# Differential attention in a four-layer network: ScalarE's order inside a unit, second exponentials ahead of the copy of turned probabilities

## The chip, the core and the metric

The kernel is one program on one core of a Trainium2 chip. The time is that of one execution on the device, in microseconds (us). The engines named here are TensorE (PE in the profile, PEld for its weight loads), VectorE (DVE), ScalarE (ACT), GpSimd (POOL) and SyncE (SP), which starts the DMA transfers. Each engine works through its own list of instructions in order; they meet only at semaphores.

## The reference, cut to what matters

The network is four layers of attention and feed-forward on x of 8 x 256 x 256 (float32), each followed by a layer norm. The change lies in the fourth attention, which is differential: two softmaxes per head, their difference weighted by lambda, and a softmax of that difference again.

```python
energy = jnp.einsum('bqhad,bkhad->bahqk', qd, kd)          # a = 0, 1; 16 heads, d = 16
energy = jnp.where(causal, NEG, energy)
scores = jax.nn.softmax(energy / np.sqrt(D), axis=-1)       # the first exponentials
...
diff = scores[:, 0] - lam * scores[:, 1]
diff = jnp.where(causal, NEG, diff)
diff = jax.nn.softmax(diff, axis=-1)                        # the second exponentials
att = jnp.einsum('bhqv,bvhd->bqhd', diff, v)
att = att * jax.lax.rsqrt(jnp.mean(att * att, axis=-1, keepdims=True) + EPS) * rms_w
```

## The kernel before, in words

The eight stages of the network run one after the other; `l3_attention` is the seventh. It goes over the 8 batch elements ("batches"). A batch is 8 units, i = 0 to 7: unit i takes the score half a = i % 2 of the four heads r = i // 2 (one head r of each of four groups g). Work is staged over units, so that each engine's list for unit i holds pieces of several units:

- TensorE, `scores(b, i)` (L1911, matmuls at L1922 and L1925): scores of unit i into the four PSUM banks S. There is one set S, so it waits on `p_exp`, which counts the first exponentials of the unit before. Then, at even i, `values` (L1939, matmuls L1946 and L1949) of a head finished earlier; then a `piece` of the next batch's projections (L1861 keys, L1868 queries, L1876 values) or, at i = 0, the output projection of two batches before (L1970); then `turn(b, i, 0)` and `turn(b, i, 1)` (L1936), which transpose the second probabilities of unit i - 4, two heads' worth, into PSUM banks PT[0] and PT[1]; then at even i `turn_back` (L1956).
- VectorE: `maxima` (L2221) of the scores, `second_maxima` (L2237), the ratios, at even i `values_out` (L2253), the rotated projections (L2182, L2185), its share of the copies, `out_of_psum` (L2248, PT[1]), at i = 6 ahead of it the norm of the batch before (`norm_2`, from L2269), and at i = 0 the addition of the projected output to x (L113).
- GpSimd: mask (L2046), `difference` (L2056, L2059) and `second_bias` (L2068), the bias nb2 of the second exponentials.
- ScalarE, per unit: `exponentials` of unit i, twice (L2113; the last one signals `p_exp`), at i = 7 `output` (L2139), then `out_of_psum` for unit i - 4 (L2124: the copy of PT[0] into `pt`, signals `pt_even`) and `second` for unit i - 3 (L2133: four second exponentials, signals `p_ready`).

Who waits for ScalarE's two signals: `turn(b, i, 0)` waits on `p_ready` of the second exponentials that ScalarE makes in unit i - 1, and also on `pt_even` of the copy that it makes in unit i - 1, since PT[0] must be free. `values(b, i)` waits on `pt_even` of the copy in unit i - 1, and not on `p_ready`. ScalarE's copy itself waits on `pt_ps` (the turn of the same unit), its second exponentials on `nb_ready` from GpSimd's L2068.

The batches are an opening (batch 0, where the copy begins at unit 4 and the second exponentials at unit 3), a second pass (batch 1), five turns of a loop (batches 2 to 6), the last batch 7, and a closing pass that has no new scores: on ScalarE copies at units 0 to 3 and second exponentials at units 0 to 2.

Of the kernel before, what the change touches and what calls it, by code (L numbers as in the profile page):

```python
# [1754 lines left out]
def l3_attention(nc, c, x_sb, mv, xT, w, psum):  # L1755
# [10 lines left out]
    with ExitStack() as ctx:  # L1766
# [71 lines left out]
        def live(i, lag, opening, closing):  # L1838

            return i >= lag if opening else i < lag if closing else True  # L1840

        def part(i):

            return slice(2 * (i % 2), 2 * (i % 2) + 2)

        with nc.Block() as block:
            @block.sync
            def _(sp):
                sp.dma_start(xc[:, :, :], xT[:, :, 0:T]).then_inc(x_staged, 16)
                with sp.Fori(0, B - 1) as b:  # L1850
                    sp.wait_ge(piece_ps, b * NQ + 10)
                    sp.dma_start(xc[:, :, :], xT[:, :, bass.ds(b * T + T, T)]).then_inc(x_staged, 16)
# [245 lines left out]
            @block.scalar  # L2098
            def _(act):
                nc.scalar.preload_act_table(ACT.Exp)  # L2100
                act.wait_ge(set_up, 2)
                nc.scalar.activation(lam[:, :, :], lam[:, :, :], ACT.Exp).then_inc(lam_ready, 1)
                act.sem_inc(pt_even, 1)

                def exponentials(b, i, pair, opening):
                    r, a = i // A, i % A
                    if pair == 0 and not opening:
                        act.wait_ge(pt_ps, b * NU * 2 + 4 * r - 12)
                    act.wait_ge(nm_ready, 2 * (b * NU + i) + pair + 1)
                    for g in range(2 * pair, 2 * pair + 2):  # L2110
                        for t in range(TT):
                            k = slice(t * P, t * P + (t + 1) * P)
                            last = nc.scalar.activation(pr[:, r, a, g, k], S[:, g, k], ACT.Exp, bias=nm[:, i % 2, g, t:t + 1],  # L2113
                                                        accum_out=sums[:, r, a, g, t:t + 1])
                    if pair == 1:
                        last.then_inc(p_exp, 1)

                def out_of_psum(b, i, opening):
                    s = b * NU + i - 4
                    r, g = (i - 4) // 2 % R, part(i - 4).start  # L2120
                    if not (opening and i - 4 < 4):
                        act.wait_ge(av_ps, b * R + (i - 4) // 2 - 1)
                    act.wait_ge(pt_ps, 2 * s + 1)
                    nc.scalar.activation(pt[:, r % 2, g, :], PT[0][:, 0:3 * P], ACT.Copy).then_inc(pt_even, 1)  # L2124

                def second(b, i):
                    s = b * NU + i - 3
                    r, heads = (i - 3) // 2 % R, part(i - 3)
                    act.wait_ge(nb_ready, s + 1)
                    for g in range(heads.start, heads.stop):  # L2130
                        for t in range(TT):
                            k = slice(t * P, t * P + (t + 1) * P)
                            last = nc.scalar.activation(pr[:, r, 1, g, k], pr[:, r, 0, g, k], ACT.Exp, bias=nb2[:, r, g, t:t + 1],  # L2133
                                                        scale=rec[:, r, 0, g, t:t + 1])
                    last.then_inc(p_ready, 1)

                def output(b):
                    act.wait_ge(oT_ps, b + 1)
                    nc.scalar.activation(oT[:, :, :], OT.rearrange("p (k t) -> p k t", k=KD), ACT.Copy).then_inc(oT_ready, 1)  # L2139

                def sequence(b, opening=False, closing=False):
                    for i in range(NU):
                        if not closing:
                            exponentials(b, i, 0, opening)
                            exponentials(b, i, 1, opening)
                        if i == 7 and not opening:
                            output(b - 1)
                        if live(i, 4, opening, closing):
                            out_of_psum(b, i, opening)
                        if live(i, 3, opening, closing):  # L2150
                            second(b, i)

                sequence(0, opening=True)
                with act.Fori(0, B - 1) as b:
                    sequence(b + 1)
                sequence(B, closing=True)

            @block.vector
# [743 lines left out]
```

## Time and profile before

| what | value |
|---|---|
| median of 3 runs | 2773.51 us (2773.32 to 2775.98) |
| the profiled execution, its own time | 2775.95 us |
| its span, first to last instruction | 2774.1 us |
| the fourth attention, first to last exponentials L2113 | 1863.3 to 2290.0 us of the span |
| the five loop batches, unit 0 to unit 0 | 54.7 us each |
| ACT, DVE, POOL busy in batch 3 (54.67 us) | 44.3, 41.1, 40.2 us |

The profiled execution's own time stands 2.4 us above the median of the runs. Times inside the trace are microseconds from the start of its span. "Idle before" names the engine whose signal ended the wait of an instruction. In a timeline a row is one or several instructions of one line in a row: start, duration, engine, line, output<-input, count, and in brackets the wait ahead of it.

### The profile page before, as it was taken

How to read it: one execution, taken by the hardware profiler on the slowest of the kernel's cores; microseconds unless marked ns; L12 is line 12 of the kernel's file. 1: busy time of each engine (PE TensorE's matmuls, PEld its weight loads, DVE VectorE, ACT ScalarE, POOL GpSimd, SP SyncE). 2: the span in 40 equal slices, each digit the busy share in tenths (PEclk: the TensorE clock that was granted, in tenths of full speed). 3: DMA queues.
4: the chain of work that ended last, by engine and by line, in shares of the span. 5: the costliest groups of instructions: out<-in, count | busy, mean ns of one | idle time of the engine just before them, and what ended most of it. 6: DMA issues, size and time to landing. Idle time of an engine off the chain costs nothing. (4 is left out here: it accounts for less than half of the span.)

```text
span 2774.1 us, 42332 instructions
## 1 busy us (share of the span) xinstructions
PE 2418.6 (87%) x13892; PEld 1890.7 (68%) x13892; DVE 1898.9 (68%) x4354; ACT 1389.3 (50%) x3744; POOL 500.6 (18%) x477
## 2 busy tenths in 40 slices
PE   6997999979999999999699788977777775999998
PEld 5665566657777777777577666855555554888887
DVE  3664588867655665566554577866777775788887
ACT  4664477765445444545322214327878783333332
POOL 2442200020000000000022100007777771000000
PEclk9998999989999999999899999989898876999999
DMA  4001000001001100110200000010000003222222
GB/s 162 11 11 62 1 1 0 0 34 35 22 12 34 34 23 11 34 34 26 110 0 0 0 0 0 1 52 5 9 4 4 4 4 140 72 64 72 70 64 59
DMA packets 43902, 88.79 MB, mean 32 GB/s; under 512 B 7328, under 2 KB 20128, under 8 KB 42272
## 3 DMA queue, kind: packets, MB, share of 16 engines
q1 hardware_dynamic: 43808, 87.58, 9.6%
q8 instruction: 54, 0.88, 0.1%
q14 instruction: 40, 0.33, 0.0%
HBM read 78.65 MB, written 2.36 MB: 29 GB/s over the span
## 5 line engine op out<-in xcount | busy, mean ns | idle before, releaser
L2113 ACT ACTIVATE l3a_pr<-psum,l3a_nm 128x128 f32<-128x128 f32 (+1 forms) x512 | 207.3, 430 | 73.3 <-DVE l3a_nm L2221 73.3
L1099 ACT ACTIVATE l1a_pr<-psum,l1a_nb,l1a_rq 128x128 f32<-128x128 f32 (+1 forms) x256 | 127.4, 510 | 80.3 <-DVE l1a_nb L1185 74.5
L2221 DVE TENSOR_REDUCE l3a_nm<-psum 128x2 f32<-128x256 f32 (+1 forms) x256 | 124.7, 549 | 54.8 <-PE psum L1925 54.5
L1361 POOL TENSOR_TENSOR l1f_acc<-l1f_t 128x512 f32<-128x512 f32 x4 | 6.3, 1571 | 838.6 <-DVE l1f_t L1427 838.6
L2513 ACT ACTIVATE l3f_sg<-psum 128x512 f32<-128x512 f32 x96 | 57.4, 598 | 193.4 <-PE psum L2465 193.4
L2463 PE MATMUL psum<-l3f_x_hi,l3f_w_hi 128*128 128x512 f32 x384 | 151.8, 395 | 1.7 <-DVE l3f_w_lo L2549 1.7
L2464 PE MATMUL psum<-l3f_x_lo,l3f_w_hi 128*128 128x512 f32 x384 | 151.5, 395 | 0.0
L2465 PE MATMUL psum<-l3f_x_hi,l3f_w_lo 128*128 128x512 f32 x384 | 150.3, 392 | 0.0
L113 DVE TENSOR_TENSOR x_sb<-psum,x_sb 128x512 f32 (+3 forms) x44 | 36.7, 833 | 162.3 <-PE psum L1038 104.9
L2046 POOL TENSOR_TENSOR l3a_pr<-l3a_pr,w_l3a_mask 128x1024 f32<-128x1024 f32 x32 | 75.5, 2360 | 316.4 <-ACT l3a_pr L2113 316.4
L372 POOL TENSOR_TENSOR l0a_pr<-l0a_pr,l0a_rec 128x256 f32<-128x256 f32 (+1 forms) x128 | 101.7, 826 | 142.6 <-DVE l0a_rec L462 142.6
L2133 ACT ACTIVATE l3a_pr<-l3a_pr,l3a_nb,l3a_rec 128x128 f32<-128x128 f32 (+1 forms) x256 | 120.2, 568 | 3.3 <-POOL l3a_nb L2068 3.3
L2497 ACT ACTIVATE l3f_w_hi<-w_l3f_all 128x768 fp32r<-128x768 f32 x96 | 81.3, 848 | 80.6 <-PE psum L2482 80.3
L1001 PE MATMUL psum<-l1a_kT,l1a_qT 128*128 128x128 f32 (+1 forms) x512 | 100.8, 342 | 22.7 <-ACT l1a_pr L1099 15.8
L1038 PE MATMUL psum<-l1a_kT,l1a_ko 128*128 128x256 f32 x512 | 112.6, 381 | 6.1 <-ACT l1a_ko L1088 6.1
L2059 POOL TENSOR_TENSOR l3a_pr<-l3a_pr 128x768 f32<-128x768 f32 x64 | 115.8, 1810 | 5.0
L2480 PE MATMUL psum<-l3f_w_hi,l3f_h_hi 128*128 128x256 f32 x384 | 109.1, 284 | 2.4 <-DVE l3f_h_lo L2599 2.4
L1038 PEld LDWEIGHTS psum<-l1a_kT,l1a_ko 128*128 128x128 f32 x512 | 96.6, 190 | 20.4 <-issue 7.6
L2113 ACT ACTIVATION_READ_ACCUMULATOR l3a_pr<-psum,l3a_nm 128x1 f32 x512 | 110.3, 215 | 0.0
L392 ACT ACTIVATE l0a_pr<-psum,l0a_nm 128x128 f32<-128x128 f32 (+1 forms) x256 | 103.6, 437 | 10.6 <-DVE l0a_nm L449 10.2
L2482 PE MATMUL psum<-l3f_w_hi,l3f_h_lo 128*128 128x256 f32 x384 | 108.9, 284 | 0.0
L2481 PE MATMUL psum<-l3f_w_lo,l3f_h_hi 128*128 128x256 f32 x384 | 108.8, 283 | 0.0
(447 smaller groups left out, 7275.2 us busy)
## 6 DMA issues: line engine op xcount, KB each, us to landing
l1a_kT<-l1a_o_dram SPq DMA_DIRECT2D x64, 256.0 KB, 2.7
l3f_cbuf<-l3f_c_rows SPq DMA_DIRECT2D x64, 192.0 KB, 2.9
w_l3f_all<-l3f_all_dram SPq DMA_DIRECT2D x1, 9216.0 KB, 24.8
l3f_cbuf<-l3f_c_rows SPq DMA_DIRECT2D x64, 128.0 KB, 3.0
w_l0f_w<-l0f_w_dram SPq DMA_DIRECT2D x2, 2048.0 KB, 10.2
l3f_cbuf<-l3f_c_rows SPq DMA_DIRECT2D x64, 64.0 KB, 2.6
w_l1f_all<-l1f_all_dram SPq DMA_DIRECT2D x1, 2560.0 KB, 8.7
cf_sb<-xT SPq DMA_DIRECT2D x9, 256.0 KB, 2.5
```

Source lines behind the costliest of these rows:

```text
L1038: last = mm(PT[0][:, t * D:(t + 1) * D], oT[:, h, t * P:(t + 1) * P], wo[:, h, :], start=(h == 0), stop=(h == H - 1))
L1099: last = nc.scalar.activation(pr[:, n % 2, i, s], S[n % 2][:, i, s], ACT.Exp, bias=nb[:, n % 2, t, i:i + 1], scale=rq[:, t, 2 * n + i:2 * ...
L2059: nc.gpsimd.tensor_tensor(pr[:, r, 0, heads, :], pr[:, r, 0, heads, :], pr[:, r, 1, heads, :], ALU.add).then_inc(dif_ready, 1)
L2113: last = nc.scalar.activation(pr[:, r, a, g, k], S[:, g, k], ACT.Exp, bias=nm[:, i % 2, g, t:t + 1], accum_out=sums[:, r, a, g, t:t + 1])
L2133: last = nc.scalar.activation(pr[:, r, 1, g, k], pr[:, r, 0, g, k], ACT.Exp, bias=nb2[:, r, g, t:t + 1], scale=rec[:, r, 0, g, t:t + 1])
L2221: last = nc.vector.tensor_reduce(nm[:, i % 2, 2 * pair:2 * pair + 2, t], S[:, 2 * pair:2 * pair + 2, t * P:t * P + (t + 1) * P], AX.X, ALU ...
L2463: mm(bk[n % 2], hi, x_hi[:, k, chunk], start=(k == 0), stop=False)
L2464: mm(bk[n % 2], hi, x_lo[:, k, chunk], start=False, stop=False)
L2465: last = mm(bk[n % 2], lo, x_hi[:, k, chunk], start=False, stop=(k == KD - 1))
L2480: mm(Y[b % 2][:, t, :], h_hi[:, n % 2, tokens], hi, start=False, stop=False)
L2481: mm(Y[b % 2][:, t, :], h_hi[:, n % 2, tokens], lo, start=False, stop=False)
L2482: last = mm(Y[b % 2][:, t, :], h_lo[:, n % 2, tokens], hi, start=False, stop=(e == NH - 1 and t % 2 == 1))
```

## The change

In each unit ScalarE's program now calls `second` ahead of `out_of_psum`. Nothing else is edited; the other engines' lists are the same as before.

```diff
                         if i == 7 and not opening:
                             output(b - 1)
+                        if live(i, 3, opening, closing):
+                            second(b, i)
                         if live(i, 4, opening, closing):
                             out_of_psum(b, i, opening)
-                        if live(i, 3, opening, closing):
-                            second(b, i)
```

ScalarE's list in a unit of the loop, the difference from before to after (l3a_pt<-psum is the copy of turned probabilities; l3a_pr<-l3a_pr,l3a_nb,l3a_rec are the second exponentials; L2122 and L2123 are the copy's waits):

```order
+L2133 ACTIVATE l3a_pr<-l3a_pr,l3a_nb,l3a_rec 128x128
+L2133 ACTIVATE l3a_pr<-l3a_pr,l3a_nb,l3a_rec 128x256
+L2133 ACTIVATE l3a_pr<-l3a_pr,l3a_nb,l3a_rec 128x128
+L2133 ACTIVATE l3a_pr<-l3a_pr,l3a_nb,l3a_rec 128x256
 L2122 REGISTER_ALU
 L2123 ISA
 L2124 ACTIVATE l3a_pt<-psum 128x384
-L2133 ACTIVATE l3a_pr<-l3a_pr,l3a_nb,l3a_rec 128x128
-L2133 ACTIVATE l3a_pr<-l3a_pr,l3a_nb,l3a_rec 128x256
-L2133 ACTIVATE l3a_pr<-l3a_pr,l3a_nb,l3a_rec 128x128
-L2133 ACTIVATE l3a_pr<-l3a_pr,l3a_nb,l3a_rec 128x256
```

The four second exponentials have moved from behind the copy to ahead of it; the copy, with its waits, now stands last in the unit.

ScalarE's list from unit 7 of the last batch into the closing pass, before (L2139 is the copy of the turned output, L2154 the end of the loop's code):

```order
L2139 ACTIVATE l3a_oT<-psum 128x512
L2124 ACTIVATE l3a_pt<-psum 128x384
L2133 ACTIVATE l3a_pr<-l3a_pr,l3a_nb,l3a_rec 128x128
L2133 ACTIVATE l3a_pr<-l3a_pr,l3a_nb,l3a_rec 128x256
L2133 ACTIVATE l3a_pr<-l3a_pr,l3a_nb,l3a_rec 128x128
L2133 ACTIVATE l3a_pr<-l3a_pr,l3a_nb,l3a_rec 128x256
L2154 REGISTER_ALU
L2154 COMPARE_AND_BRANCH
L2124 ACTIVATE l3a_pt<-psum 128x384
```

The same place in the changed kernel:

```order
L2139 ACTIVATE l3a_oT<-psum 128x512
L2133 ACTIVATE l3a_pr<-l3a_pr,l3a_nb,l3a_rec 128x128
L2133 ACTIVATE l3a_pr<-l3a_pr,l3a_nb,l3a_rec 128x256
L2133 ACTIVATE l3a_pr<-l3a_pr,l3a_nb,l3a_rec 128x128
L2133 ACTIVATE l3a_pr<-l3a_pr,l3a_nb,l3a_rec 128x256
L2124 ACTIVATE l3a_pt<-psum 128x384
L2154 REGISTER_ALU
L2154 COMPARE_AND_BRANCH
L2133 ACTIVATE l3a_pr<-l3a_pr,l3a_nb,l3a_rec 128x128
```

At the seam the copy of unit 7 now stands behind four second exponentials, and the closing pass begins with second exponentials and not with a copy.

## Rows read from the trace of the kernel before

**Rows 1.** The page: the span.

```profile
span 2774.1 us, 42332 instructions
```

**Rows 2.** Waits between 1880 and 2310 us: waiter, releaser: total us, times, longest.

```profile
ACT l3a_pr L2113 <- DVE l3a_nm L2221: 57.3, 59, 3.1
...
ACT l3a_pt L2124 <- PE psum L1936: 22.0, 17, 3.9
PE psum L1922 <- ACT l3a_pr L2113: 22.0, 18, 3.2
```

**Rows 3.** Stretches batch by batch (3 and 5): length, busy times, clock, DMA.

```profile
2021.75:2076.42 54.67, 41.29 (x349) 29.34 (x350) 41.12 (x104) 44.30 (x170) 40.15 (x38) 0.91 0.01 5
...
2131.12:2185.77 54.65, 44.07 (x349) 31.46 (x350) 41.19 (x104) 44.30 (x169) 40.19 (x38) 0.84 0.01 5
```

**Rows 4.** Timeline, batch 4, end of unit 1 to unit 2, full clock.

```profile
2085.79 0.20 POOL L2068 TENSOR_TENSOR l3a_nb<-l3a_nm,l3a_rec 128x4 f32<-128x4 f32 x1
2085.80 0.53 ACT L2124 ACTIVATE l3a_pt<-psum 128x384 f32<-128x384 f32 x1
2086.17 1.89 ACT L2133 ACTIVATE l3a_pr<-l3a_pr,l3a_nb,l3a_rec 128x128 f32<-128x128 f32 x4
...
2087.41 0.64 PE L1946 MATMUL psum<-l3a_pt,l3a_va 128*32 128x256 f32 x8
...
2090.03 0.82 PE L1936 MATMUL psum<-cf_sb,l3a_pr 128*128 128x128 f32 x6
...
2092.54 0.55 DVE L2248 COPY l3a_pt<-psum 128x384 f32<-128x384 f32 x1
...
2092.75 0.43 PE L1956 MATMUL psum<-cf_sb,l3a_ots 128*128 128x128 f32 x2 [1.90 <-DVE l3a_k L2182]
```

**Rows 5.** Timeline, batch 5, the same place, half clock.

```profile
2143.32 3.21 PE L1861 MATMUL psum<-xT,w_l3a_k 128*128 x8
...
2146.37 0.82 PE L1936 MATMUL psum<-cf_sb,l3a_pr 128*128 128x128 f32 x6
...
2147.45 0.43 PE L1956 MATMUL psum<-cf_sb,l3a_ots 128*128 128x128 f32 x2 [0.26 <-DVE l3a_k L2182]
```

**Rows 6.** Timeline, end of unit 5: batch 1, last row batch 7.

```profile
1950.27 1.86 ACT L2133 ACTIVATE l3a_pr<-l3a_pr,l3a_nb,l3a_rec 128x128 f32<-128x128 f32 x4 [1.06 <-POOL l3a_nb L2068]
...
1950.39 0.64 PE L1946 MATMUL psum<-l3a_pt,l3a_va 128*32 128x256 f32 x8
...
1952.04 0.35 ACT L2113 ACTIVATE l3a_pr<-psum,l3a_nm 128x128 f32<-128x128 f32 x1
...
2278.34 1.87 ACT L2133 ACTIVATE l3a_pr<-l3a_pr,l3a_nb,l3a_rec 128x128 f32<-128x128 f32 x4 [0.84 <-POOL l3a_nb L2068]
```

**Rows 7.** Timeline, unit 7 of the last batch and the closing pass.

```profile
2290.41 0.54 ACT L2124 ACTIVATE l3a_pt<-psum 128x384 f32<-128x384 f32 x1
...
2291.05 1.08 PE L1946 MATMUL psum<-l3a_pt,l3a_va 128*32 128x256 f32 x8 [2.84 <-ACT l3a_pt L2124]
...
2296.24 0.69 DVE L113 TENSOR_TENSOR x_sb<-psum,x_sb 128x512 f32<-128x512 f32 x1 [3.20 <-PE psum L1970]
...
2297.44 1.00 DVE L2237 TENSOR_REDUCE l3a_nm<-l3a_pr 128x2 f32<-128x256 f32 x2
...
2298.70 0.20 POOL L2068 TENSOR_TENSOR l3a_nb<-l3a_nm,l3a_rec 128x4 f32<-128x4 f32 x1
...
2304.79 0.88 PE L1936 MATMUL psum<-cf_sb,l3a_pr 128*128 128x128 f32 x6 [1.37 <-ACT l3a_pr L2133]
```

**Rows 8.** Stretches unit by unit: units 5 and 7 of batches 3, 5.

```profile
2055.26:2061.41 6.15, 6.12 (x56) 4.64 (x56) 4.88 (x11) 5.57 (x21) 5.47 (x5) 0.85 0.12 43
...
2068.43:2076.42 7.99, 5.99 (x46) 3.79 (x46) 4.24 (x10) 5.93 (x23) 6.00 (x5) 0.79 0.00 0
...
2164.64:2172.40 7.76, 7.76 (x56) 5.83 (x56) 4.94 (x11) 5.57 (x22) 5.46 (x5) 0.67 0.10 34
...
2179.42:2185.77 6.35, 5.05 (x50) 3.33 (x49) 4.23 (x10) 5.93 (x22) 6.02 (x5) 0.96 0.00 0
```

## The prediction

> **What bounds the kernel now.** I read the page first, for the span [rows 1]; the change touches only the fourth attention, about a sixth of it, so I read the rest there. Next the waits of that stretch [rows 2]. They show a ring: nearly every unit's exponentials L2113 wait for VectorE's maxima L2221 (59 waits, 57.3 us), VectorE waits for TensorE's scores, and these wait for ScalarE's exponentials only in 18 cases (22.0 us on the matmuls). In most other units TensorE comes to `scores` late through its own list. Third, the stretches by batch [rows 3]: a loop batch lasts 54.7 us, in which ScalarE is busy 44.3 us and every other engine less, so nobody is full. The time is a ring of signals, and what counts is not how much ScalarE does but when its two signals come. Last I read the timeline unit by unit, which gives the ends of the waits.
>
> One unit of ScalarE's tail, in [rows 4]: the copy starts at 2085.80, the second exponentials at 2086.17, that is 0.37 later (the copy's 0.53 overlaps the next start), and they last 1.89. So the tail is 0.37 + 1.89 = 2.26 us after the exponentials end, in either order. Before, `pt_even` comes at +0.53 and `p_ready` at +2.26. After, `p_ready` comes at +1.89 and `pt_even` at about +2.26: roughly 1.7 us later, and later still where the bias of GpSimd is not there.
>
> **The change part by part.** No instruction is added or removed; five per unit change places, and no DMA is among them.
>
> What could gain. `turn(b, i, 0)` needs both signals of the unit before, so it starts at the end of the tail in either order; 0.37 us of earlier `p_ready` is worth nothing. The other gain is where the copy sat waiting for its turn: 22.0 us in 17 waits [rows 2], mostly in units 3 and 5. Now the second exponentials fill that time. But the next exponentials wait for VectorE's maxima, and those for scores that TensorE issues behind its projections and turns, none of which waits for ScalarE there. So the tail ends sooner and ScalarE waits longer at L2113. I take 0 us; the bound is 22.0, if everything behind moved with it.
>
> What can lose. `values` at even units needs only `pt_even`. In [rows 4] it starts at 2087.41. After: the tail starts at 2085.80, but the bias L2068 ends at 2085.99, so the second exponentials start near 2086.04, and the copy ends 2.26 later, 2088.3. `values` slips by 0.9 us, and so do the keys and turns behind it: the turn that starts at 2090.03 and lasts 0.82 would end near 2091.8. VectorE takes it up only at 2092.54, and `turn_back` at 2092.75 waits for VectorE's L2182. So 0.7 us of slack is left and the slip is swallowed: 0 us in batches 1 to 4. What is late next is only TensorE's own keys.
>
> In batches 5 and 6 the same place runs at the lower clock: eight key matmuls take 3.21 us, turn starts at 2146.37, and `turn_back` follows after a wait of only 0.26 [rows 5]. A slip of 0.9 meets that 0.26 of idle, and about 0.2 comes back because the shifted keys run partly past the slow stretch. About 0.45 us stays, twice: 0.9 us. The bounds are 0, and 0.9 in each of the batches 1 to 6, 5.4 us, if the slack is not there.
>
> In unit 5 of batch 1 ScalarE is late through GpSimd: the copy ran ahead and then the second exponentials waited 1.06 us for the bias, from 1950.27 for 1.86 us, and the next exponentials start at 1952.04 without a wait [rows 6]. Now the copy comes behind them, so it adds its 0.37 to the path: the exponentials of unit 6 start 0.4 us later. `values` slips from 1950.39 to about 1952.6, by 2.2, but VectorE reads its result only later. I take 0.4 us (0 to 2.2). Batch 7 has the same case [rows 6], with the lower clock a little behind it, so the turns of unit 6 may hold up VectorE's norm as well: 0.6 us (0.4 to 2.0).
>
> The closing pass has no exponentials to hide behind. At its head `values` waits 2.84 us for the copy of unit 7, which starts at 2290.41 and lasts 0.54, and goes at 2291.05 [rows 7]. Moved behind the second exponentials, that copy ends at 2290.41 + 2.26 = 2292.7, and `values` starts 1.7 us later, and with it the output projection and VectorE's addition L113 at 2296.24. Some comes back: the second exponentials that `turn` waits for in unit 1 of this pass stood behind a copy that waited for the turn of unit 0; in the new order they are made while TensorE still projects. What then comes last is VectorE's list behind L113. L113 moves to 2297.9, the second maxima L2237 start 1.2 us after it and the bias L2068 starts 1.26 after those [rows 7], so this bias is ready at about 2300.6. Two tails of 2.26 follow, to 2305.1, and up to 0.5 for the last bias, 2305.6. The last turn, which needs the second of these tails, started at 2304.79 [rows 7], so the end comes 0.3 to 0.8 later. I take 0.8 us, the last bias being behind VectorE's whole list (bounds 0 and 1.7, nothing given back).
>
> The sum: 0.9 + 0.4 + 0.6 + 0.8 = 2.7 us. On the profiled execution that is 2775.95 + 2.7 = 2778.65; this execution stood 2.4 above the median, so for the median 2773.51 + 2.7 = 2776.2 us. All lower bounds give 2773.9, all upper ones 5.4 + 2.2 + 2.0 + 1.7 = 11.3, so 2784.8. What a measurement of this kernel tells from no change is about 0.2%, 5.5 us.
>
> **A rule weighed.** The rows show that the lower clock matters by place. Batch 3 had a granted clock of 0.91 and batch 5 one of 0.84, and they last 54.67 and 54.65 us [rows 3]: equal, because in batch 3 unit 7 was slow (7.99 us at 0.79) and unit 5 fast (6.15 at 0.85), and in batch 5 unit 7 fast (6.35 at 0.96) and unit 5 slow (7.76 at 0.67) [rows 8]. One slow stretch on the path costs 1.6 us and each batch has one. The Trainium skill, "TensorE: Matmul & The Clock Gate", section "HAM oscillation — how this bites in real kernels", says that matmuls which keep pausing for something fall back to the half clock, over and over. By that rule the new pause ahead of `values` speaks against the change, and each loop batch could catch a second slow stretch, which would give the result of the second rival below; by the rows a pause moves slow stretches more than it adds them.
>
> **The rivals.**
> 1. *The `values` slip is not swallowed* (slower). The slack of 0.7 us in [rows 4] holds only if VectorE's list there stays late. If it does not, the upper end of that term counts, 5.4 + 0.4 + 0.6 + 0.8 = 7.2: 2780.7 us. For it: 0.26 us in [rows 5]. Against: 1.90 us of wait in [rows 4].
> 2. *Two slow stretches a batch* (slower): 1.6 us in each of five loop batches, 8.0 on top of 1.8: 2783.3 us. For it: longer pauses of TensorE. Against: batches 3 and 5 traded one for the other.
> 3. *No slow stretch on the path* (faster): the slip moves TensorE's bursts so that the lower clock falls on neither unit 5 nor unit 7: 1.6 us less in each of five batches, 2773.5 + 1.8 - 8.0 = 2767.3 us. It decides from 5 of 5 batches on, since with 4 (6.4 less 1.8) the gain is under 5.5 us.
> 4. *The whole is hidden*: the closing pass gets back at its turns what it lost at its head and the rest is under the maxima's waits: 2773.5 us. The change then does nothing.
>
> **How the numbers follow.** The forecast 0.60; rival 1 has 0.11, rival 2 0.12, rival 3 0.09, rival 4 0.08. The forecast's own range is 2774 to 2779. The forecast and rival 4 are within 0.2% (0.68), rivals 1 and 2 slower (0.23), rival 3 faster (0.09). The range for 8 in 10 goes from 2770 (halfway into rival 3, two or three batches) to 2783, up to rival 2.
>
> **What would show it in the profile after.** The waits of L2124 for L1936 nearly gone in the loop (from 22.0 us to a few), and the waits of L2113 for L2221 longer, or less if the units grew; new waits of L1946 for L2124, of 0.9 us at unit 2 in each batch and 2.2 us at unit 6 of batch 1; `turn_back` at unit 2 at the same distance from the exponentials as before; unit 5 of batch 1 longer by 0.4 us; the first `values` of the closing pass waiting 1.7 us more, and its last turn 0.8 us later. Wrong would be: a loop batch that no longer lasts 54.7 us, either way.

## The result, and the profile after

The changed kernel takes 2782.11 us, median of 19 runs (2775.44 to 2786.7), the one before 2774.86 (19 runs, 2763.33 to 2780.23). The ratio is 1.0026 with an interval of 1.0018 to 1.0034: slower by 7.2 us, 5.0 to 9.4. The forecast was 2776.2, a change of 2.7 us and with it most of the chance on "within 0.2%". The range and the sign hold. The size does not, and 0.26% lies outside the "within 0.2%" that had 0.68 of the chance.

The profiled execution of the changed kernel has this span, 4.7 us above [rows 1]:

```profile
span 2778.8 us, 42332 instructions
```

The waits in the fourth attention, the changed kernel, 1880 to 2315 us (waiter, releaser: total us, times, longest):

```profile
ACT l3a_pr L2113 <- DVE l3a_nm L2221: 72.6, 53, 3.0
...
PE psum L1922 <- ACT l3a_pr L2113: 23.3, 18, 3.3
...
PE psum L1946 <- ACT l3a_pt L2124: 21.4, 14, 5.9
...
ACT l3a_pr L2133 <- POOL l3a_nb L2068: 9.2, 10, 1.8
...
ACT l3a_pt L2124 <- PE psum L1936: 6.9, 4, 4.0
```

Against [rows 2]: the copy's wait for its turn went from 22.0 us to 6.9, and ScalarE's wait for the maxima from 57.3 to 72.6. The idle time of ScalarE was mostly moved. New is the third row: `values` L1946 waits 21.4 us for the copy (in the same view of before 2.8 us, once).

Where the time went is seen in the lengths of batches, from the start of the first exponentials L2113 of one batch to those of the next, read from the timelines of both (batch 7 up to the start of its last unit):

| us | batch 0 | 1 | 2 | 3 | 4 | 5 | 6 | 7 | whole, to the end of the last L2113 | from there to the last L113 |
|---|---|---|---|---|---|---|---|---|---|---|
| before | 50.67 | 53.02 | 54.73 | 54.67 | 54.70 | 54.65 | 54.64 | 46.34 | 426.75 | 30.05 |
| changed | 50.68 | 55.95 | 55.48 | 54.99 | 53.71 | 55.28 | 56.33 | 49.36 | 435.11 | 30.12 |

The exponentials' part is 8.4 us longer, 2.9 of them in batch 1, 2.4 in the loop, 3.0 in batch 7. The closing pass, where the forecast put 0.8, is not longer by more than 0.1. No loop batch but batch 3 is still within 0.5 us of 54.7, which is the sign of being wrong that the prediction named. The stages ahead of this one took 3.2 us less in this execution, which the change doesn't touch.

Unit 2, batch 3, of the changed kernel, first the timeline:

```profile
2033.58 0.46 ACT L2124 ACTIVATE l3a_pt<-psum 128x384 f32<-128x384 f32 x1
2034.09 1.08 PE L1946 MATMUL psum<-l3a_pt,l3a_va 128*32 128x256 f32 x8 [0.80 <-ACT l3a_pt L2124]
...
2035.53 3.78 PE L1861 MATMUL psum<-xT,w_l3a_k 128*128 x8
...
2039.11 1.39 PE L1936 MATMUL psum<-cf_sb,l3a_pr 128*128 128x128 f32 x6
...
2040.33 0.38 PE L1956 MATMUL psum<-cf_sb,l3a_ots 128*128 128x128 f32 x2
```

then that unit and the whole batch as stretches (length, busy times, granted clock, DMA):

```profile
2035.06:2043.00 7.94, 7.94 (x53) 6.09 (x46) 4.97 (x13) 5.44 (x22) 5.53 (x7) 0.67 0.00 0
...
2022.21:2077.20 54.99, 43.01 (x365) 30.62 (x358) 41.36 (x104) 44.24 (x169) 40.16 (x38) 0.88 0.01 5
```

`values` waits about the forecast pause (0.80 us). But then `values`, the keys and the turns run at the lower of TensorE's two levels, 1.2 and not 2.4 GHz: the keys take 3.78 us, the turns 1.39 and not 0.82 as in [rows 4], and unit 2 is 7.94 us long at a clock of 0.67. Only `turn_back` (0.38 us) is at the high level again. The same unit in the kernel before:

```profile
2034.61:2040.78 6.17, 4.28 (x38) 3.26 (x37) 4.77 (x13) 5.44 (x22) 3.85 (x5) 1.00 0.00 0
```

The Trainium skill, "TensorE: Matmul & The Clock Gate", section "HAM oscillation — how this bites in real kernels", tells of matmuls that pause for a transfer in every step of a loop and fall back to the half clock each time; its waits are several times as long as this one. The trace agrees in that a low clock goes with the new pause. It does not show the pause as the whole reason. In batch 4 the new pause is the 0.75 us before 2089.09, and the clock had fallen at 2088.0 already, as the row of `values` and two stretches ahead of it show:

```profile
2089.09 1.08 PE L1946 MATMUL psum<-l3a_pt,l3a_va 128*32 128x256 f32 x8 [0.75 <-ACT l3a_pt L2124]
```

```profile
2087.00:2088.00 1.00, 1.00 (x20) 0.62 (x16) 0.81 (x5) 1.00 (x3) 1.00 (x1) 1.00 0.00 0
2088.10:2089.00 0.90, 0.24 (x2) 0.00 (x0) 0.90 (x1) 0.90 (x3) 0.90 (x1) 0.50 0.00 0
```

What differs is how long it stayed low. In batches 3, 4 and 6 it stayed low through the keys (3.78 us) and into the turns. In batches 2 and 5 it was back during the keys (3.13 and 2.88 us), as it was in the kernel before in batches 5 and 6 (3.21 and 3.17), where unit 2 lasted 6.17 and 6.18 us all the same.

A second thing shows in unit 5 of batch 5, the changed kernel:

```profile
2168.20 0.20 POOL L2068 TENSOR_TENSOR l3a_nb<-l3a_nm,l3a_rec 128x4 f32<-128x4 f32 x1
...
2168.44 1.86 ACT L2133 ACTIVATE l3a_pr<-l3a_pr,l3a_nb,l3a_rec 128x128 f32<-128x128 f32 x4 [1.45 <-POOL l3a_nb L2068]
2170.21 0.47 ACT L2124 ACTIVATE l3a_pt<-psum 128x384 f32<-128x384 f32 x1
2170.73 1.08 PE L1946 MATMUL psum<-l3a_pt,l3a_va 128*32 128x256 f32 x8 [2.20 <-ACT l3a_pt L2124]
...
2172.17 1.54 PE L1936 MATMUL psum<-cf_sb,l3a_pr 128*128 128x128 f32 x6
...
2173.82 0.20 DVE L2269 TENSOR_SCALAR psum<-l3a_vv 128x32 int32<-128x32 int32 x1 [1.09 <-PE psum L1936]
```

The bias from GpSimd is late, the second exponentials wait 1.45 us for it, the copy stands behind them, `values` waits 2.20, the turns run at the low clock, and VectorE's norm L2269, which is queued ahead of the next maxima, waits 1.09 for the turn. The forecast had this chain in batches 1 and 7 only. In batch 1 of the changed kernel it did not come: units 4, 5 and 6 last 7.34, 5.83 and 7.21 us there, against 5.88, 6.54 and 6.65 before.

The seam and the closing pass, changed kernel (against [rows 7]):

```profile
2295.54 1.89 ACT L2133 ACTIVATE l3a_pr<-l3a_pr,l3a_nb,l3a_rec 128x128 f32<-128x128 f32 x4
...
2297.29 0.52 ACT L2124 ACTIVATE l3a_pt<-psum 128x384 f32<-128x384 f32 x1
...
2297.91 1.08 PE L1946 MATMUL psum<-l3a_pt,l3a_va 128*32 128x256 f32 x8 [5.95 <-ACT l3a_pt L2124]
...
2310.85 0.84 PE L1936 MATMUL psum<-cf_sb,l3a_pr 128*128 128x128 f32 x6 [0.93 <-ACT l3a_pt L2124]
...
2312.50 0.64 PE L1946 MATMUL psum<-l3a_pt,l3a_va 128*32 128x256 f32 x8 [0.81 <-DVE l3a_pt L2248]
```

### The profile page after: what moved, and what is told of

It is laid out like the page before. It is cut to its first block and busy times, and to the rows that moved or that the text cites. A ratio compares the mean times of both kernels' runs of the same rounds, so it can differ in the third digit from the quotient of the medians.

```text
span 2778.8 us, 42332 instructions
## 1 busy us (share of the span) xinstructions
PE 2417.4 (87%) x13892; PEld 1888.0 (68%) x13892; DVE 1900.3 (68%) x4354; ACT 1387.8 (50%) x3744; POOL 500.6 (18%) x477
## 5 line engine op out<-in xcount | busy, mean ns | idle before, releaser
L2113 ACT ACTIVATE l3a_pr<-psum,l3a_nm 128x128 f32<-128x128 f32 (+1 forms) x512 | 207.0, 429 | 91.7 <-DVE l3a_nm L2221 91.7
L2513 ACT ACTIVATE l3f_sg<-psum 128x512 f32<-128x512 f32 x96 | 57.3, 597 | 192.5 <-PE psum L2465 192.5
L113 DVE TENSOR_TENSOR x_sb<-psum,x_sb 128x512 f32 (+3 forms) x44 | 36.7, 834 | 161.2 <-PE psum L1038 104.9
L2113 ACT ACTIVATION_READ_ACCUMULATOR l3a_pr<-psum,l3a_nm 128x1 f32 x512 | 110.5, 216 | 0.0
```

## The experiments

All times are medians; a ratio is against runs of the kernel before on the same chip. A "part" is the time from the first to the last L2113 in the run's own profile, 426.75 us before and 435.11 changed. It is read from one execution, and in some kernels it does not say the same as the median. Unit lengths are distances between first exponentials.

**Which units.** ScalarE's program asks in each unit which call comes first; the condition is the only difference between the four kernels (`i % 2 == 1`, `i % 2 == 0`, `i == 1`, `i != 1`).

```diff
+                        first = i % 2 == 1
+                        if first and live(i, 3, opening, closing):
+                            second(b, i)
                         if live(i, 4, opening, closing):
                             out_of_psum(b, i, opening)
-                        if live(i, 3, opening, closing):
+                        if not first and live(i, 3, opening, closing):
                             second(b, i)
```

Odd units:

> Second exponentials ahead of the copy in odd units only (1, 3, 5, 7), as before in even ones. The copies whose signal the next unit's values wait for are just those of the odd units. Theory A, the later pt_even delays values at even units and above all at unit 2: the whole loss stays, +6 to +9 us against the kernel before. Theory B, it is the order in general (ScalarE's tail, in every unit): about half, +3 to +4 us.

Even units:

> Second exponentials ahead of the copy in even units only. The copies of even units gate only the turn of the next unit, which needs both signals anyway. Theory A: no change, within 2 us of the kernel before. Theory B, the order in general: about half of the loss, +3 to +4 us.

Unit 1 alone:

> Second exponentials ahead of the copy in unit 1 of each batch alone. Theory A with its place (unit 1 to 2, where TensorE goes on to the keys): +4 to +8 us, the larger part of the loss; the keys of unit 2 run at the lower clock in most batches and unit 2 lasts over 6.9 us in place of 6.2. Theory C, the loss is in units 5 and 7, where GpSimd's bias is late and the copy is put on the path: within 2 us of the kernel before.

All but unit 1:

> Second exponentials ahead of the copy in every unit but unit 1. Theory A with its place: 0 to +3 us, only the terms of unit 5 in batches 1 and 7 (1 us together) and of the closing pass are left. Theory C: the whole loss, +6 to +9 us.

| kernel | median | ratio (interval) | part |
|---|---|---|---|
| odd units | 2783.98 | 1.0038 (1.0024 to 1.0052) | 435.11 |
| even units | 2772.53 | 0.9992 (0.9983 to 1.0001) | 426.77 |
| unit 1 alone | 2770.44 | 0.9987 (0.9978 to 0.9996) | 423.20 |
| all but unit 1 | 2780.63 | 1.0019 (1.0010 to 1.0028) | 428.73 |

The first two rule out theory B: the odd swap repeats the changed kernel batch by batch (55.95, 55.46, 54.99, 53.73, 55.26, 56.32, 49.37 us from batch 1 on), the even swap the kernel before (53.01, 54.74, 54.69, 54.70, 54.65, 54.64, 46.35). Only the copies whose signal `values` waits for count. The last two contradict the place I had given: by the ratios, unit 1 swapped alone makes the kernel 3.6 us faster, and without it 5.3 us of loss remain. The unit lengths say why in part. With unit 1 alone, unit 2 is long as forecast in batches 2 to 5 (6.85, 7.83, 7.94, 7.84 us), but not in batch 6, where the same pause costs nothing:

```profile
2191.77 0.64 PE L1946 MATMUL psum<-l3a_pt,l3a_va 128*32 128x256 f32 x8 [0.83 <-ACT l3a_pt L2124]
...
2192.55 1.99 PE L1861 MATMUL psum<-xT,w_l3a_k 128*128 x8
```

and unit 2 as a stretch:

```profile
2192.73:2198.91 6.18, 5.20 (x41) 4.07 (x42) 4.78 (x13) 5.45 (x21) 3.85 (x5) 1.00 0.00 0
```

A pause of 0.83 us stands ahead of `values`, the clock is 1.00 and unit 2 lasts 6.18 us. So a pause of this length does not always bring the low clock. And in the loop the slow stretches in units 4 and 5 are missing or shorter (in batch 4, 6.59 and 5.85 in place of 7.38 and 7.80). The parts do not add up: -3.55 with unit 1 alone and +1.98 with the rest do not make +8.36. In the kernel without unit 1 the part (+1.98) also says less than the ratio (5.3 us); in its profiled execution the stages behind this attention took 5.8 us more than before, so where the remaining loss lies is not shown.

**The wait alone, on TensorE.** ScalarE as before; `values` waits for the signal that comes last.

```diff
                         if done:
...
+                            if turning:
+                                pe.wait_ge(p_ready, b * NU + i - 3)
                             values(b, i)
```

> ScalarE's order as in the kernel before; TensorE's values alone waits, at even units, also for p_ready of ScalarE's unit before, the signal that now comes last. Theory A, all of the loss comes from the later start of values: as the changed kernel, +6 to +9 us, with the same unit lengths. Rival, the loss is ScalarE's (the copy put behind a late bias, the copy on the path to the next exponentials): under +3 us.

Median 2780.37, ratio 1.0024 (1.0011 to 1.0037): 5.4 us slower (medians), within the interval as much as theory A wanted. But its profiled execution, 2776.9 us, is among the fastest of its 12 runs (2771.57 to 2787.5), its part is 425.26 us, shorter than before, and the unit lengths are not those of the changed kernel; from the end of the part to the last L113 it took 33.51 and not 30.05. Unit 2 is long as in theory A (8.11, 6.93, 7.83, 7.14, 7.91 us in the loop). The run supports that the wait on TensorE is enough to cost something; where it costs in the slower runs, no trace shows.

**Pause or delay.** Two kernels with the same six extra transposes of the unit matrix ahead of `values` at unit 2, in the changed kernel, where they fill the pause, and in the kernel before, where they only delay `values`.

```diff
+                            if i == 2:
+                                for _ in range(6):
+                                    nc.tensor.transpose(OT[:, T:T + P], c["id"], c["id"])
                             values(b, i)
```

Changed kernel, filled:

> The changed kernel with six extra transposes of the unit matrix ahead of values at unit 2 (about 0.8 us of matmul in place of the wait; extra work, the output is not touched by it). Clock theory: with the pause filled the keys run at the full clock, unit 2 is back near 6.2 us in most batches, and the time changes by more than 3 us against the changed kernel, in a direction that the order of slow stretches in the later units decides. Rival, a plain delay: unit 2 stays at 6.9 to 7.9 us and the time is that of the changed kernel, +6 to +9 us on the one before.

Kernel before, delayed:

> The kernel before with the same six transposes ahead of values at unit 2: a delay of values by 0.8 us without a pause. Clock theory: unit 2 stays at about 6.2 us, the slack in front of turn_back takes the delay, within 2 us of the kernel before. Rival, a plain delay of 0.8 us is enough to lengthen unit 2: unit 2 at 6.9 us or more in the loop and +3 us or more.

Filled, the changed kernel takes 2775.89 us, ratio 1.0001 (0.9992 to 1.0010), part 428.16; the delayed one 2774.33, 0.9997 (0.9987 to 1.0007), part 426.75, every batch within 0.03 us of before. Unit 2 of batch 3 in the filled kernel, the timeline (L1990 are the extra transposes):

```profile
2034.24 0.82 PE L1990 MATMUL psum<-cf_sb 128*128 128x128 f32 x6
2035.22 0.64 PE L1946 MATMUL psum<-l3a_pt,l3a_va 128*32 128x256 f32 x8 [0.17 <-ACT l3a_pt L2127]
...
2036.01 2.00 PE L1861 MATMUL psum<-xT,w_l3a_k 128*128 x8
2037.84 0.82 PE L1936 MATMUL psum<-cf_sb,l3a_pr 128*128 128x128 f32 x6
...
2039.66 0.43 PE L1956 MATMUL psum<-cf_sb,l3a_ots 128*128 128x128 f32 x2 [0.99 <-DVE l3a_k L2185]
```

and that unit as a stretch:

```profile
2036.20:2042.38 6.18, 5.18 (x41) 4.06 (x41) 4.78 (x13) 5.44 (x22) 3.85 (x5) 1.00 0.00 0
```

The keys take 2.00 us and not 3.78, the clock is 1.00, and `turn_back` has 0.99 us of the slack that the forecast counted on. The loop batches are 54.59 to 54.64 us long again. So the delay of `values` costs nothing at unit 2 in the loop, as forecast (0.9 us of it here, 0.65 in the delayed kernel); the pause does, through the clock. 7.0 of the 8.4 us of the part go with it. In batch 1 unit 2 still takes 7.31 us in place of 6.09. What stays is 1.4 us, in batch 7 (47.74 us against 46.34), where units 5 and 6 last 6.69 and 7.68 us against 6.32 and 6.64. There the late bias sits ahead of the copy, and the norm behind the turn, as in batch 5 above:

```profile
2279.70 1.86 ACT L2136 ACTIVATE l3a_pr<-l3a_pr,l3a_nb,l3a_rec 128x128 f32<-128x128 f32 x4 [1.23 <-POOL l3a_nb L2071]
2281.47 0.47 ACT L2127 ACTIVATE l3a_pt<-psum 128x384 f32<-128x384 f32 x1
2282.04 1.08 PE L1946 MATMUL psum<-l3a_pt,l3a_va 128*32 128x256 f32 x8 [1.94 <-issue]
...
2285.13 0.19 DVE L2272 TENSOR_SCALAR psum<-l3a_vv 128x32 int32<-128x32 int32 x1 [1.10 <-PE psum L1936]
```

(L2136, L2127 and L2272 are the second exponentials, the copy and the norm there.)

**Keys ahead of `values`.** In the changed kernel the `piece` of unit 2 is called before `values`.

```diff
+                        if i == 2 and not closing:
+                            piece(b, i, opening, more)
                         if done:
...
-                        if not closing and i < 7:
+                        if not closing and i < 7 and i != 2:
                             piece(b, i, opening, more)
```

> The changed kernel with TensorE's key projection of unit 2 moved ahead of values, so that the wait for the copy is spent on matmuls. Theory A with the clock (the pause ahead of the keys brings the half clock into unit 2): unit 2 back to 6.2 us, and the kernel within 3 us of the kernel before or faster. Rival, the pause at unit 2 is not what costs, since that unit alone came out 3.6 us faster: no nearer to the kernel before than +5 us.

2773.82 us, ratio 0.9997 (0.9988 to 1.0006), part 425.81. Unit 2 is 6.17 to 6.18 us in all loop batches. This removes the loss without extra work, as theory A with the clock wanted. The keys are no longer behind the copy here, so this kernel takes away the delay as well as the pause; it is the filled and the delayed kernel that tell the two apart. Its loop batches together are 2.8 us shorter than before and batch 7 is 2.4 longer; neither was forecast.

**Single units 5 and 7.** The condition of the first four kernels, with `i == 5` and `i == 7`.

Unit 5 alone:

> Second exponentials ahead of the copy in unit 5 alone. By the prediction's terms: unit 5 to 6 of batches 1 and 7 longer by 0.4 and 0.6 us, nothing in the loop: within 2 us of the kernel before. Rival, odd units other than 1 carry the loss (the kernel with all but unit 1 swapped stood 5.3 us above): +3 us or more, and units 6 and 7 of the loop batches longer.

Unit 7 alone:

> Second exponentials ahead of the copy in unit 7 alone, the last batch's included, so that the closing pass starts with a late copy but keeps its own order. Prediction's term: the first values of the closing pass 1.7 us later, of which little comes back when the pass keeps the old order: +1.5 us. Clock rival: the pause ahead of values at unit 0 moves slow stretches in the loop: batches of other lengths than 54.7 us, by 1 us or more each.

Unit 5 alone: 2777.25 us, ratio 1.0015 (1.0003 to 1.0028). The ratio says 4.2 us slower, with 0.8 as its lower end, the medians 2.5 (2774.75 before): that leans to the rival and does not settle it, for in the profiled execution (2771.21 us, the lowest of its 12 runs) the part is 424.99, shorter than before; batch 7 is longer by 1.4 (47.77), and batch 1 by 2.15 (55.17). Unit 7 alone: 2772.53, 0.9993 (0.9980 to 1.0006): no loss, and 30.01 us from the part's end to the last L113. The forecast 1.5 us for the seam is not in the total, though the last turn of the closing pass comes 0.9 us later after the part's end (15.57 us against 14.71). The clock rival came true in two of the five loop batches: batches 2 and 3 last 52.57 and 53.45 us, the others 54.65 to 54.70.

**Filling the waits ahead of `turn_back`.** If slow stretches follow pauses, the kernel before has some to give back. Extra transposes of the unit matrix go in front of `turn_back`:

```diff
+                            for _ in range((0, 0, 8, 0, 12, 0, 10, 0)[i]):
+                                nc.tensor.transpose(OB[:, T:T + P], c["id"], c["id"])
                             turn_back(b, i)
```

In the kernel before:

> The kernel before with extra transposes of the unit matrix ahead of turn_back (8, 12 and 10 at units 2, 4 and 6, about 1.1 to 1.6 us), where TensorE waits 1.9 to 2.5 us for VectorE; extra work that the output does not see. Clock theory, slow stretches follow pauses: units 4, 5 and 7 lose slow stretches, the stage is 3 to 10 us shorter, the kernel faster than the one before. Rival, the slow stretches are not the pauses' doing: no change or, where a filler is too long, slower by 1 to 3 us.

In the changed kernel, with the filler of unit 2 as well:

> The changed kernel with both fillers, ahead of values at unit 2 and ahead of turn_back at units 2, 4 and 6. Clock theory: the same as the kernel before with the turn_back fillers, within 3 us, since the order on ScalarE then costs nothing. Rival: +5 us and more above that one.

The first takes 2764.34 us, ratio 0.9965 (0.9950 to 0.9980): 10 us faster than the kernel before, part 416.45. The second takes 2779.82, 1.0019 (1.0008 to 1.0031), part 428.27. Unit 4 of batch 3 in the kernel before, then batch 3, its unit 4 and its unit 5, in the first, as stretches:

```profile
2047.87:2055.26 7.39, 4.92 (x33) 3.54 (x33) 4.46 (x13) 5.44 (x21) 5.05 (x6) 0.66 0.00 0
...
2015.36:2067.60 52.24, 42.60 (x379) 31.40 (x380) 41.10 (x104) 44.14 (x170) 40.15 (x38) 0.93 0.01 5
2042.30:2048.11 5.81, 4.75 (x49) 3.98 (x49) 4.46 (x13) 5.44 (x21) 3.48 (x4) 1.00 0.00 0
2048.11:2054.72 6.61, 4.67 (x50) 3.17 (x49) 5.72 (x13) 5.47 (x21) 6.53 (x7) 1.00 0.11 40
```

Unit 4 falls from 7.39 us (clock 0.66) to 5.81 (1.00) in every loop batch, and unit 6 from 7.02 to 6.15. Unit 2 pays 0.8. Its filler does not fill the wait: `turn_back` waits there for VectorE's keys, and the edit put the transposes behind that wait. In batch 2 (L2015 are the transposes, L2184 the keys):

```profile
1979.73 1.09 PE L2015 MATMUL psum<-cf_sb 128*128 128x128 f32 x8 [1.83 <-DVE l3a_k L2184]
1980.66 0.38 PE L1956 MATMUL psum<-cf_sb,l3a_ots 128*128 128x128 f32 x2
```

The wait of 1.83 us stands ahead of them, and `turn_back` goes 0.93 us late. At units 4 and 6 the fillers begin right behind the turns and take the place of the wait. The second kernel has the same unit 4, 5.82 us, and yet loses in units 5 and 6 (6.97 and 8.26 against 6.61 and 6.15 in batch 3). The timelines of unit 5, batch 3. The first kernel (L2126 the copy, L2135 the second exponentials, L2271 the norm):

```profile
2051.29 0.53 ACT L2126 ACTIVATE l3a_pt<-psum 128x384 f32<-128x384 f32 x1
...
2052.90 0.64 PE L1946 MATMUL psum<-l3a_pt,l3a_va 128*32 128x256 f32 x8
2052.95 1.86 ACT L2135 ACTIVATE l3a_pr<-l3a_pr,l3a_nb,l3a_rec 128x128 f32<-128x128 f32 x4 [1.13 <-POOL l3a_nb L2070]
...
2056.49 0.18 DVE L2271 TENSOR_SCALAR psum<-l3a_vv 128x32 int32<-128x32 int32 x1
```

The second (L2138 the second exponentials, L2129 the copy, L2274 the norm):

```profile
2056.99 1.86 ACT L2138 ACTIVATE l3a_pr<-l3a_pr,l3a_nb,l3a_rec 128x128 f32<-128x128 f32 x4 [1.51 <-POOL l3a_nb L2073]
2058.76 0.47 ACT L2129 ACTIVATE l3a_pt<-psum 128x384 f32<-128x384 f32 x1
2059.28 1.08 PE L1946 MATMUL psum<-l3a_pt,l3a_va 128*32 128x256 f32 x8 [2.26 <-ACT l3a_pt L2129]
...
2062.37 0.20 DVE L2274 TENSOR_SCALAR psum<-l3a_vv 128x32 int32<-128x32 int32 x1 [1.09 <-PE psum L1936]
```

With the old order the copy runs while the bias is still on its way, and `values` does not wait. With the new one it waits 2.26 us. In both the bias is late and unit 4 is short (5.81 and 5.82 us). So the expectation that the order then costs nothing was wrong: with the waits filled, the swap costs 15.5 us by the medians, 11.8 by the parts.

## Why the prediction was right or wrong

The number of the prediction lay inside its range, but mostly not for its reasons, and that is luck. The 7.2 us measured are even the sum of rival 1, whose mechanism, a delay that meets no slack, the filled and the delayed kernel refute. What happened is rival 2 in kind (more low clock), though the loop cost 2.4 us and not its 8.0.

- *No gain from the copy's waits (0 us).* Right: 22.0 us of waits became 6.9, and ScalarE waited 15.3 more for the maxima.
- *Only copies that gate `values` matter.* Right, shown by the odd and even kernels, which are in the exponentials' part the changed kernel and the kernel before over again. Their closing passes differ, see below.
- *The slip at unit 2 "is swallowed: 0 us in batches 1 to 4".* This is the step that failed. The slack is there (delay alone: no change; 0.99 us of it is left in the filled kernel, where I had counted 0.7 in all), but I worked out the keys behind the slip at full clock. With the pause the keys ran at the low clock: unit 2 is 6.93 to 7.94 us in the loop and 8.79 in batch 1, against 6.1 to 6.2. I had the mechanism as the second rival, with the Trainium skill's rule beside it, and argued against it with "a pause moves slow stretches more than it adds them". Half of that held: in batches 3 to 6 units 4 and 5 gave time back (batch 4 is 1.0 us shorter than before). Term by term, the loop cost 2.4 us, where 0.9 were forecast for it. The count of slow stretches was off too: I had one a batch, but unit 4, 7.38 or 7.39 us long in every loop batch (clock 0.66 in batch 3), was another.
- *Unit 5 of batches 1 and 7, 0.4 and 0.6 us.* Right in mechanism, too small, and too narrow in place. With unit 5 alone swapped, unit 5 of batch 1 is 0.4 us longer as forecast (6.91 against 6.54), but units 6 and 7 behind it another 1.8. Batch 7 measured 1.4 us in the filled kernel, where nothing else was left (bounds given: 0.4 to 2.0). Missed was that the bias is late in loop batches too once their unit 4 is short, so that a batch which wins 1.5 us in unit 4 pays it in units 5 and 6: 5.88, 6.91 and 7.62 us in batch 5 of the changed kernel, where unit 1 alone swapped leaves 5.89, 6.54 and 6.65 in batch 2.
- *The closing pass, 0.8 us.* The first steps came as worked out. From the start of the tail (2290.41 before, 2295.54 now) `values` begins 2.37 us on in place of 0.64, and the last turn 15.31 in place of 14.38, 0.9 later. But the `values` behind it ran at the high clock, 0.64 us against 1.08 before, and the last L113 comes 29.79 us after the start of the tail in place of 29.72: 0.1 us is left. This is two effects that cancel. From the end of the part to the last L113 the odd kernel takes 31.92 us and the even one 28.26, against 30.05 before: the odd swap alone costs 1.9, above my upper bound of 1.7, and the even swap alone gives back 1.8. Half of that comes before the last turn (13.78 us after the part's end in place of 14.71) and half behind it, where the clock is 0.70 and not 0.55, as the stretches from the last turn to the last L113 show, before and in the even kernel:

```profile
2304.79:2320.13 15.34, 7.87 (x36) 4.81 (x36) 4.62 (x15) 1.09 (x2) 1.09 (x1) 0.55 0.00 1
...
2310.07:2324.55 14.48, 7.01 (x36) 4.54 (x36) 4.62 (x16) 1.09 (x2) 1.09 (x1) 0.70 0.00 1
```
- *The third rival, slow stretches off units 5 and 7.* Not this change, but the filler kernel did it at unit 4 and gained 10 us.

The account of the profiled pair: the part +8.36, the closing pass up to the last L113 +0.07, the stages ahead -3.23, the rest -0.50, together +4.70.

Open stays why the slow stretches fall where they do once the pattern is moved: why unit 1 alone wins 3.6 us is seen in part (units 4 and 5 are faster) and not explained, and so is why its pause costs a slow unit 2 in four loop batches and nothing in the fifth. Open too is in which units the slower runs of the TensorE wait kernel and of unit 5 alone lose, since the profiled execution of each is one of the fast ones. That unit 0 of batch 1 is 0.95 us shorter whenever unit 7 is swapped was seen and not followed up.

## What to carry to other kernels

Before reordering an engine's list, write down for each of its signals who waits for that one alone: the swap gave the signal that was needed at the end of the tail anyway a lead, and put off by 1.7 us the one that another engine used at once. Put work whose input may be late behind work that is ready. And cost a new pause on TensorE by what may run at the lower clock around it, not by its length alone; where TensorE must wait, filling the wait with matmuls, or calling an independent projection first, can be worth more than the wait. A filler has to stand ahead of the wait; behind it, it is only a delay.

## What the runs showed of the hardware

At unit 2 a pause goes with a low clock and a delay without idle time does not. With 0.80 us of new idle time ahead of `values`, eight key matmuls took 3.78 us (clock 0.67); with six transposes in that place, 2.00 us (1.00). The pause is no rule by itself: in the kernel with unit 1 alone the keys took 1.99 us behind a pause of 0.83 (batch 6), and in batch 4 of the changed kernel the clock fell 0.3 us before the pause began. Fillers of 1.1 to 1.6 us in front of `turn_back` raised batch 3 from 0.91 to 0.93 and shortened it by 2.4 us (0.7 to 2.9 in the five loop batches), although they add 240 matmuls to the program; at unit 4 the clock went from 0.66 to 1.00. The placement repeats closely where the order of the signals is the same: the odd kernel and the changed one agree in every batch within 0.02 us, though their parts start 0.4 us apart in the trace, and the delayed kernel and the one before within 0.03. The even kernel and the one before agree within 0.02, with parts that start 6.2 us apart.
